# Key bias written into PSUM by ScalarE, key sums of two tiles per GpSimd operation, context splits in alternate steps: first stage of a fused two-layer Perceiver kernel

## What is computed

```
def feature_map(x, scale):
    x = relu(x) + 1e-6
    x = x / scale
    n = norm(x); xp = x ** 3
    return xp / norm(xp) * n
k = feature_map(ctx @ Wk + bk, softplus(scale))
q = feature_map(layernorm(x) @ Wq + bq, softplus(scale))
z = 1 / (q . k.sum(over context) + 1e-6)      # per head of 32 columns
kv = k^T (ctx @ Wv + bv)                       # per head
out = (q kv) * z
```

## Time and profile before

| | |
|---|---|
| median of 3 runs | 1933.73 us (1933.23 to 1936.25) |
| profiled execution, its own time | 1940.93 us |
| its span | 1939.6 us |
| TensorE busy | 1770.8 us, 91% |
| VectorE busy | 1246.0 us, 64% |
| ScalarE busy | 948.3 us, 49% |
| GpSimd busy | 443.8 us, 23% |
| last value product of the first stage starts | 448.9 us |

### The profile page before, as it was taken

How to read it: one execution, slowest core, us unless ns; L and a number is a source line. 1 busy time by engine, 2 the same in 40 slices (tenths; PEclk the granted TensorE clock), 3 DMA queues, 4 the chain that set the end, 5 groups by cost and what they waited for, 6 DMA issues and landing times.

```text
span 1939.6 us, 25860 instructions
## 1 busy us (share of the span) xinstructions
PE 1770.8 (91%) x9438; PEld 1443.4 (74%) x9438; DVE 1246.0 (64%) x2521; ACT 948.3 (49%) x1969; POOL 443.8 (23%) x262
## 2 busy tenths in 40 slices
PE   6899999997999889999999999998888869889896
PEld 4667787875878679999899898885555547668685
DVE  6888989884543426667677667996343365665653
ACT  4444545451244225556566556884222345565552
POOL 1444545451000012113111311221111011221221
PEclk9999999998999999999999999998899979999998
DMA  6122222213720399777677767686200356776721
GB/s 231 65 87 88 88 87 87 87 44 130 266 77 1 104 287 317 233 234 241 194 228 232 238 197 198 183 221 234 103 6 6 120 177 209 246 271 198 244 76 61
DMA packets 147134, 310.03 MB, mean 160 GB/s; under 512 B 11472, under 2 KB 100816, under 8 KB 135440
## 3 DMA queue, kind: packets, MB, share of 16 engines
q1 hardware_dynamic: 145072, 301.85, 47.6%
q0 software_dynamic: 1920, 6.36, 1.0%
HBM read 226.88 MB, written 81.28 MB: 159 GB/s over the span
## 4 chain that ended last, share of the span: by engine, by line
PE 68%; DVE 20%; DMA 4%; ACT 4%; issue 2%; POOL 0%; SPq 0%; DVEq 0%; ACTq 0%; POOLq 0%
PE bank L99 11%; PE bank L100 10%; PE bank L101 10%; PE bank L1309 5%; PE bank L1087 4%; PE bank L1620 4%; PE bank L1621 4%; PE bank L1624 4%; DVE PTL L1094 2%; PE bank L1042 2%; DVE TT L1044 2%; PE bank L1113 2%; PE bank L1114 2%; DVE CNL L424 2%; DMA HG<-tmp_xd,IDX 2%
## 5 line engine op out<-in xcount | busy, mean ns | idle before, releaser
L1094 DVE TENSOR_TENSOR PTL<-bank,PTH 128x512 fp32r<-128x512 f32 x256 | 175.9, 687 | 94.6 <-ACT PTH L1092 93.4
L1092 ACT CAST PTH<-bank 128x512 fp32r<-128x512 f32 x256 | 149.8, 585 | 166.2 <-PE bank L1087 166.2
L1607 DVE TENSOR_TENSOR WS<-EW,WS 128x1024 fp32r<-128x1024 f32 (+1 forms) x120 | 150.4, 1263 | 74.5 <-ACT WS L1604 74.2
L1072 ACT ACTIVATE TT<-TT,MX 128x512 f32<-128x512 f32 x256 | 186.5, 729 | 8.6 <-DVE MX L1062 8.6
L1044 DVE CUSTOM_DVE_ANT_0 TT<-bank,MASK 128x512 f32<-128x512 f32 x256 | 174.0, 681 | 7.8 <-POOL MASK L1025 5.8
L1604 ACT CAST WS<-EW 128x1024 fp32r<-128x1024 f32 (+1 forms) x144 | 139.4, 977 | 52.2 <-PE bank L1624 47.9
L1087 PE MATMUL bank<-IDN,TT 128*128 128x128 f32 x1024 | 155.1, 274 | 4.0 <-DVE RS L1137 2.9
L99 PE MATMUL bank<-BCH,WKT 128*128 128x256 f32 x512 | 149.9, 293 | 6.0 <-DVE BCL L606 5.2
L100 PE MATMUL bank<-BCL,WKT 128*128 128x256 f32 x512 | 146.2, 286 | 0.0
L101 PE MATMUL bank<-BCH,WKT 128*128 128x256 f32 x512 | 146.2, 286 | 0.0
L464 POOL TENSOR_TENSOR KS<-KS,FH 128x512 f32<-128x512 f32 x60 | 100.8, 1680 | 196.9 <-DVE FL L454 196.7
(11 more groups left out here) (291 smaller groups left out, 4607.9 us busy)
## 6 DMA issues: line engine op xcount, KB each, us to landing
EW<-in_ewg SPq DMA_DIRECT2D x48, 1024.0 KB, 6.3
KST<-tmp_k SPq DMA_DIRECT2D x43, 768.0 KB, 5.7
tmp_k<-EKH SPq DMA_DIRECT2D x128, 256.0 KB, 2.8
EW<-in_ewg SPq DMA_DIRECT2D x24, 768.0 KB, 4.8
CT<-in_ctxT SPq DMA_DIRECT2D x32, 512.0 KB, 4.3
CN<-in_ctxN SPq DMA_DIRECT2D x32, 512.0 KB, 3.3
BCT<-in_ctxT SPq DMA_DIRECT2D x32, 512.0 KB, 3.4
tmp_k<-EKL SPq DMA_DIRECT2D x64, 256.0 KB, 2.8
```

The source lines that it names most:

```text
L1072: t_e[(n, kc)] = tick("act", act.activation(TT[:, sl, cs], TT[:, sl, cs], ACT.Exp, bias=MX[:, n % 4, 5:6], scale=SC1, accum_out=SUM[:, b % ...
L1094: t = free[bk] = tick("dve", dve.tensor_tensor(PTL[:, q], bank[bk][:], f(PTH[:, q]), ALU.subtract))
L1607: t_lo = tick(low, E[low].tensor_tensor(WS[:, s, 1, 0:n * w], src, f(WS[:, s, 0, 0:n * w]), ALU.subtract))
```

## The change

Five edits, all in the first stage.

1. The key bias is no longer added by VectorE. ScalarE copies BK into bank i % 2 before the products of tile i (`bias_first`, for tile i + 2 at the end of `Feature(i)`), and all products of the tile add to what stands in the bank. Ahead of the loop TensorE writes each of the two banks twice with products of ONES and IDN. The maximum and the scaling then read the bank. BK's transfer is issued ahead of the first context tile's, and its 1e-6 is added early.
2. The product of the two sums in `ratio` becomes the scale of ScalarE's root.
3. GpSimd sums two tiles with each operation, 1024 columns wide, in even steps (`key_sum`), into a KS of two parts; `finish_l0` adds the parts with two products.
4. VectorE makes CTL in even steps and CNL in odd ones, both ahead of `scale_low`; ScalarE's high halves and the transfers move accordingly, with CT one group further ahead.
5. FB has three buffers in place of five, and the query blocks begin in steps 1, 5, 9 and 13.

```diff
-        FB = R("FB", [128, NF + 1, 512])
+        FB = R("FB", [128, 3, 512])
...
-        KS2 = R("KS2", [128, 2, 512])
-        KS = KS2[:, 0]
+        KS2 = R("KS2", [128, 2, 2, 512])
...
-        dma("sp", "lds", IDN[:], I["idn"])
-        dma("sp", "lds", ONES[:], I["ones"])
+        dma("sp", "ld1", IDN[:], I["idn"])
+        t_one = dma("sp", "ld1", ONES[:], I["ones"])
         t_s = dma("sp", "lds", SC, I["L0scale"])
         t_wk = [dma("sp", "ldw00", KV2[:, 0], I["L0k"][:, 0])]
+        t_b = dma("sp", "ldb0", BK[:], I["L0bk"])
         t_ct = [dma("sp", "ldct0", CT[:, 0], I["ctxT"][0]), None]
...
-        t_b = dma("sp", "ldb0", BK[:], I["L0bk"])
...
+        need("pe", t_one)
+        for bk in (0, 1, 0, 1):
+            m = pe.matmul(bank[bk][:].rearrange("p (a c) -> p a c", a=4), ONES[:],
+                          IDN[:].unsqueeze(1).broadcast_to([128, 4, 128]), start=True, stop=True)
+        free[0] = free[1] = tick("pe", m)
+        t_pre = [None, None]
+
+        def bias_first(i):
+            bk = i % 2
+            if i < 64:
+                need("act", t_bk, free[bk])
+                t_pre[bk] = tick("act", act.copy(bank[bk][:], BK[:]))
+
         need("dve", t_u)
         t = step(W, U, 1.0, None, ALU.add)
+        need("dve", t_b)
+        t_bk = tick("dve", dve.tensor_scalar(BK[:], BK[:], 1e-6, None, ALU.add))
+        bias_first(0)
         need("act", t)
         t_ln = tick("act", act.activation(L, W, ACT.Ln))
         for c in range(1, 4):
             split_wk(c)
+        bias_first(1)
         split_wk_low(0)
...
-        need("dve", t_b)
-        t_bk = tick("dve", dve.tensor_scalar(BK[:], BK[:], 1e-6, None, ALU.add))
...
-                need("dve", t_mm, t_inv, t_bk if i < 64 else t_bq[0], fa_free[s])
-                t = free[bk] = tick("dve", dve.tensor_tensor(FA[:, s], bank[bk][:], (BK if i < 64 else BQ)[:], ALU.add))
-                need("dve", t)
-                t = tick("dve", dve.scalar_tensor_tensor(out=FA[:, s], in0=FA[:, s], scalar=1e-6, in1=INV[:],
+                need("dve", t_mm, t_inv, *fa_free[s])
+                x = bank[bk][:]
+                if i >= 64:
+                    need("dve", t_bq[0])
+                    t = free[bk] = tick("dve", dve.tensor_tensor(FA[:, s], x, BQ[:], ALU.add))
+                    need("dve", t)
+                    x = FA[:, s]
+                t = tick("dve", dve.scalar_tensor_tensor(out=FA[:, s], in0=x, scalar=1e-6, in1=INV[:],
                                                          op0=ALU.max, op1=ALU.mult))
-                need("act", t, fb_free[s])
-                self.t_f2 = tick("act", act.activation(FB[:, s], FA[:, s], ACT.Square, accum_out=S1[:, i:i + 1]))
+                if i < 64:
+                    free[bk] = t
+                w = self.w = i % 2 if i < 64 else 2
+                need("act", t, fb_free[w])
+                self.t_f2 = tick("act", act.activation(FB[:, w], FA[:, s], ACT.Square, accum_out=S1[:, i:i + 1]))
...
+                t_f3 = tick("dve", dve.tensor_tensor(FA[:, s], FA[:, s], FB[:, self.w], ALU.mult))
                 need("act", t_f3)
-                self.t_s2 = tick("act", act.activation(FB[:, s], FA[:, s], ACT.Square, accum_out=S2[:, i:i + 1]))
-                fb_free[s] = self.t_s2
+                self.t_s2 = tick("act", act.activation(FB[:, self.w], FA[:, s], ACT.Square, accum_out=S2[:, i:i + 1]))
+                fb_free[self.w] = self.t_s2
...
                 t = tick("dve", dve.reciprocal(S2[:, i:i + 1], S2[:, i:i + 1]))
-                need("dve", t)
-                t = tick("dve", dve.tensor_tensor(S2[:, i:i + 1], S2[:, i:i + 1], S1[:, i:i + 1], ALU.mult))
                 need("act", t)
-                self.t_r = tick("act", act.activation(RR[:, i:i + 1], S2[:, i:i + 1], ACT.Sqrt))
+                self.t_r = tick("act", act.activation(RR[:, i:i + 1], S2[:, i:i + 1], ACT.Sqrt, scale=S1[:, i:i + 1]))
...
-            need("pe", t_ch[s], free[bk])
+            need("pe", t_ch[s], t_pre[bk])
...
-                m = mm3(bank[bk][:], a, (WKH[:, c], WKL[:, c]), c == 0, c == 3)
+                m = mm3(bank[bk][:], a, (WKH[:, c], WKL[:, c]), False, c == 3, skip=True)
...
-            need("act", F.t_r, *fh_free[s])
+            need("act", F.t_r, *fh_free[s], fh_summed[s // 2])
...
+            need("dve", F.t_hi, *fh_free[s], fh_summed[s // 2])
...
+            F.t_lo = t_lo
+
+        fh_summed = [None] * 2
+
+        def key_sum(F):
+            i, s = F.i - 1, (F.i - 1) % NF
             kb = (i // 16) % 2
             KS = KS2[:, kb]
             if i % 16 == 0:
-                need("pool", t_lo, ks_free[kb])
-                t = tick("pool", pool.tensor_tensor(KS, f(FH[:, s]), f(FL[:, s]), ALU.add))
+                need("pool", F.t_lo, ks_free[kb])
+                t = tick("pool", pool.tensor_tensor(KS, f(FH[:, s:s + 2]), f(FL[:, s:s + 2]), ALU.add))
             else:
-                need("pool", t_lo, ks_t[kb])
-                t = tick("pool", pool.tensor_tensor(KS, KS, f(FH[:, s]), ALU.add))
+                need("pool", F.t_lo, ks_t[kb])
+                t = tick("pool", pool.tensor_tensor(KS, KS, f(FH[:, s:s + 2]), ALU.add))
                 need("pool", t)
-                t = tick("pool", pool.tensor_tensor(KS, KS, f(FL[:, s]), ALU.add))
+                t = tick("pool", pool.tensor_tensor(KS, KS, f(FL[:, s:s + 2]), ALU.add))
             ks_t[kb] = t
-            F.t_ks = t
-            F.t_lo = t_lo
+            fh_summed[s // 2] = t
...
-            fh_free[s] = [t, F.t_ks]
+            fh_free[s] = [t]
...
-            t_kb = tick("pe", pe.matmul(bank[3][:], ONES[:], KS2[:, b % 2], start=True, stop=True))
+            pe.matmul(bank[3][:], ONES[:], KS2[:, b % 2, 0], start=True, stop=False)
+            t_kb = tick("pe", pe.matmul(bank[3][:], ONES[:], KS2[:, b % 2, 1], start=False, stop=True))
...
-            if i < 16 and i % 4 == 0:
+            if i < 16 and i % 4 == 1:
                 side.append(q_side(i // 4))
             if i < 64:
                 tile = ktile(i)
             if i == 0:
                 t_inv = spread_scale()
+                load_ct(2)
+                split_high(by_ct, 1)
             g = i // 2
             if 0 <= i - 3 < 64:
                 scale_high(F[i - 3])
-            if i % 2 == 0:
-                split_high(by_ct, g + 1)
-                load_ct(g + 2)
             if 0 <= i - 2 < 64:
                 F[i - 2].ratio()
-            if i % 2:
+            if i % 2 == 0:
                 split_low(by_ct, g + 1)
+                load_ct(g + 3)
+            elif i >= 3:
+                split_low(by_cn, g - 1)
+                load_cn(g + 1)
             if 0 <= i - 3 < 64:
                 scale_low(F[i - 3])
+                if i % 2 == 0:
+                    key_sum(F[i - 3])
             if 0 <= i - 1 < 64:
                 F[i - 1].cube()
             if i < 64:
                 F[i] = Feature(*tile)
+                bias_first(i + 2)
             if 0 <= i - 4 < 64:
                 t_kv = kvtile(F[i - 4])
                 if (i - 4) % 16 == 15:
...
-            if i % 2 == 0 and i >= 2:
+            if i % 2:
+                split_high(by_ct, g + 2)
+            elif i >= 2:
                 split_high(by_cn, g - 1)
-            if i % 2 and i >= 3:
-                split_low(by_cn, g - 1)
-                load_cn(g + 1)
```

10 lines of the change are left out of this document (4 added, 6 removed).

## The result

| | before | changed |
|---|---|---|
| median | 1933.48 us (4 runs, 1932.97 to 1936.25) | 1946.53 us (4 runs, 1944.72 to 1949.23) |
| ratio to before, 95% interval | | 1.0065 (1.0043 to 1.0087) |
| profiled execution's span | 1939.6 us | 1943.4 us |

The change makes the kernel 13 us slower, where 26 us faster was forecast. The spans of the two profiled executions differ by only 3.8 us, because that of before was 7.4 us above its median. In the profiles of the other kernels it takes 1482.7 to 1495.1, whatever was changed ahead of it (the kernel with the sums left out aside), so the other 5 us of the medians' 13 can't be placed.

The account below looks back on a forecast made before the run. TensorE was taken to bound the first stage, kept waiting by VectorE. Terms -5.4 + 17.4 + 12.9 + 1.1 = 26.0 us gained, so 1908 us from a median of 1933.73; range 1900 to 1921 us.

Parts of the forecast that it names:

- What bounds the kernel and the floors: First stage: TensorE's supply bounds it; floors 96.2 us for steps 5 to 20, 251.7 us for steps 20 to 63.
- the first stretch: Steps 5 to 20, 114.6 us before: most TensorE waits go, 17.4 us gained.
- Start: Before step 5: products put first and a split behind its transfer delay step 5 to 47.3 us, 5.4 us lost.
- The single costs: First-stage operations: bias write 0.6 us, maximum and scale 0.69 us, wide add 2.40 us holding VectorE about 2.3 us.
- rival (d): Slower: wide adds hold the ports longer than their unhindered time, at 3.36 us a 12.6 us round; near 1962 us, chance 0.06.
- VectorE's round: Two steps on VectorE: 6.8 us of work plus 3.7 us held by GpSimd, 10.5 us, under TensorE's 10.9.
- Lateness at a finish: Around a batch's finish VectorE's lateness peaks at 3 to 4 us, below the 5.7 us allowed, so most waits go.
- +12.9: Steps 20 to 63: gain of 16.5 us less 2.6 for extra key-sum products less 1.0, 12.9 us.
- End of the stage: After tile 63: last value products about 2 us sooner, one more key-sum product 0.86 us; 1.1 us gained.
- The term for the root: ScalarE: the wider square root replaces a 0.16 us operation and costs nothing of its own.
- The rule on the ports: VectorE and GpSimd share an exclusive lock held for the whole instruction, making wide adds worse: 10.5 us a round, not 9.6.

Follow-up runs that it names:

- sums left out: Changed kernel with GpSimd's key sums dropped except each batch's first pair; 2048.4 us, a total that says nothing since later stages compute from another sum.
- narrow sums: Changed kernel with key sums one tile per GpSimd add again, 512 columns instead of 1024; 1905.1 us, ratio to before 0.9857.
- high half first: Changed kernel with ScalarE's context high half ahead of the tile's square and bias write in each step; 1935.6 us, ratio to before 1.0007.
- apart: Changed kernel with a pair's two wide adds one step apart, FH's in the even step, FL's in the odd (last pair of a batch together); 1909.4 us.
- old order: Kernel before with only the key sums changed: two tiles per GpSimd add, two key-sum products per finish; 1946.1 us, ratio to before 1.0054.
- two shorter starts: 512-column key sums, two products first, later first bias write, earlier first norm: 1901.4 us; also copying turned rows first in step 2: 1899.4 us.

## Why the prediction was wrong

*What bounds the kernel and the floors: right; the first stretch: right in its number, in part by luck.* Step 20 starts at 144.62 us (forecast: from 47.3, 114.6 - 17.4 later, at 144.5). The stretch is 98.16 us, the 2.26 us waits of the earlier trace rows are gone and the clock is 1.00. But VectorE is late here too: narrow sums run the stretch in 95.17 us (1 us under the floor of 96.2 that the prediction worked out), and step 20 in 10.99 in place of 17.50. The bill for these steps falls due just behind the boundary, in step 20. The floor that the prediction worked out for steps 20 to 63 (251.7 and 2.6 for the extra products) is 254.3, and the kernel with narrow sums runs it in 254.44.

*Start: right within a microsecond.* -5.4 forecast, -4.54 measured (46.46 against 41.92), along the path that was walked: split of pair 2 behind its transfer at 28.56, root at 30.91, transposes at 31.95, tile 3 at 32.72. One size was off: the four products ahead take 5.09 and not 7 us.

*The single costs: right.* Bias write 0.575 us (0.6), maximum and scale 0.68 (0.69), wide add 2.39 us (2.40) and no hold longer than that. So the condition of rival (d), a hold of 2.9 us, was not met.

*VectorE's round: the step that failed.* The prediction had "Sum 6.8 + 3.7 = 10.5 us, under TensorE's 10.9". That walk took VectorE's inputs for ready. They aren't: with splits ahead of the low half and high halves at the end of the step, each split waits for two squares, bias write and high half on ScalarE, 1.91 us, and each reciprocal 0.19 for its square. The round is 2 x 3.25 (work, forecast 2 x 3.4) + 2 x 2.10 (ScalarE) + 1.72 (hold, forecast 3.7) = 12.4 us. The cube's end, the maximum and the wait hide the first wide add wholly (220.72 to 223.51, no operation is longer for it) and the wait the second for half a microsecond; the rest of the second is the hold. The loop alone would fit (2 x 5.35 = 10.7 us under 10.88), and so would the holds alone by the forecast; the prediction counted one of the two, and a margin of 0.4 us became a deficit of 1.55 per round. The ScalarE part of the prediction looked at its busy time (3.7 of 5.44 us a step) and at the chain to the next bias write, not at what VectorE's own next operation needs from it.

*Lateness at a finish: failed too.* "Around a finish ... it peaks at 3 to 4. Neither reaches 5.7" measured lateness against the bias write alone. At a batch end the limit is another: the copies that empty banks 4 to 7, two of which stand on ScalarE's queue behind work that waits for VectorE. Eight rounds of 1.55 make 12.4 us a batch. From step 21 to 37 the changed kernel takes 267.63 - 162.12 = 105.5 us and that with narrow sums 247.26 - 153.50 = 93.8: 11.7 us lost of 12.4, and 11.9 in the next batch. Within the second batch only two steps take 7.00 us (TensorE has used up its lead by then and waits for the low half and CNL); the rest, 8.4 us, falls on the batch end. The row of one of the two:
```profile
227.78 0.51 PE L99 MATMUL bank<-FH,CNH 128*128 128x512 f32 x1 [1.22 <-DVE FL L473]
```
From step 20 to 63 this makes -16.5 us in place of +12.9.

*End of the stage:* +1.1 forecast, 3.4 us lost (454.44 - 429.38 = 25.06 us from step 63 on, before 21.63). With narrow sums it is 17.05, so the wide adds cost 8.0 us here.

*Sum to the last value product:* -4.54 + 16.44 - 16.54 - 3.43 = -8.07, the 8.06 us between 446.38 and 454.44. The medians differ by 13, of which 5 can't be placed, as said above.

*The term for the root.* The prediction let the wider root cost nothing of its own. It takes 0.28 us in place of 0.20, and no plain round shows a wait for it.

*What the rest of the change gave.* With narrow sums, all other edits in place, the kernel is 1.4% faster than before, close to the 26 us forecast for the whole. The floors of the prediction apply once VectorE's round really is the shorter one; the sum counted on that with wide adds in the round, and there it was wrong.

*The rule on the ports.* The longer row of CNL (2.95 against 1.23) and, in the kernel with the high half first, the longer add of GpSimd (3.26 against 2.39), which waits for VectorE's split before it holds the low half, show that each holds the other. The Trainium skill (SBUF — State Buffer, section SBUF: two separate sides) calls this an exclusive lock that whichever engine starts first holds for its whole instruction. The traces agree in both directions, with the numbers just given. The prediction used the rule and still got the sign wrong: what a hold costs depends on what VectorE would have done meanwhile.

What is shown: the loss is that of two wide adds in a row (narrow: -41 us; apart: -37 us). That the loop through ScalarE sets how much they cost is read from the timelines and borne out by two kernels (high half first: hold and wait trade places; old order: 10 us lost and not 41). No kernel here has the old order with the bias written first. Not settled too: how much of the 8.4 us at a batch end is the half clock by itself; no kernel here kept the wait and the full clock. And by the ratios the gain of the two shorter starts over narrow sums alone is not clear of the noise.

## What to carry to other kernels

Before a margin on a round is believed, walk it through every engine in it: for each operation of the walked engine ask what it reads and where that producer stands in its own queue, above all when an edit moves both. Helper work that holds another engine off (here adds on GpSimd) was free where it fitted into a wait or beside an operation that reads a bank, so try to split it into pieces that fit before merging it into fewer long ones. If a round is longer than the bound engine's by a little, look for the payment at the next place without slack (here the emptying of the accumulators at a batch's end), where it is paid in full and with a slower clock on top.
